# Four-pass graph network, 8-head pass: ScalarE weighs eight of sixteen tiles, and tail and query products stand elsewhere in TensorE's order

## The chip, the cores and the metric

The kernel runs on one core of a Trainium2 chip. The metric is the device time in microseconds of one execution, as a median of runs. Engines are named as in the profile: PE is TensorE (PEld its weight loads), DVE is VectorE, ACT is ScalarE, POOL is GpSimd, SP is SyncE.

## What is computed

Four graph layers in a row over 6250 nodes with 256 features and 106250 edges, sorted by destination. Each is followed by a residual sum and a layer norm. The second layer, which the change touches, is an 8-head attention over the edges (`q`, `k`, `v` are projections of the node features, `c` the destination and `r` the source of an edge):

```python
qe, ke, ve = q[:, c, :], k[:, r, :], v[:, r, :]
sim = jnp.einsum('hed,hed->eh', qe, ke) * scale
m = jax.ops.segment_max(sim, c, num_segments=bs)
p = jnp.exp(sim - m[c])
s = jax.ops.segment_sum(p, c, num_segments=bs)
attn = p / s[c]
out_e = attn.T[..., None] * ve
agg = jax.ops.segment_sum(out_e, c, num_segments=bs)
```

## The kernel before

The edges lie in 880 tiles of 128, each tile with destinations in one block of 128 nodes. Five passes (`L` = 0 to 4) go over the tiles; pass 1 is the 8-head pass. It takes the tiles in 55 batches of 16. The loop body of every engine is written out for two batches, and each body does two things: the scores of batch b ("scores"), and the weighted sums of batch c = b - 1 ("sums"). Each engine runs its instructions in the order of its body; semaphores tie the engines together. There is no planner.

What a batch needs, engine by engine:

- GpSimd gathers key and value rows (`kv_t`, 512 numbers) by edge source into `ring`, 16 tiles to a set, two sets; four tiles at a time, once TensorE has summed the four tiles that lay there.
- SyncE loads mask rows (`mk`, `srow`), the destinations as a row (`relx`), and query rows of the destination block, 128 x 256 bf16 (64 KB) a tile, into eight buffers `qw`. Tiles 8 to 11 of a batch are asked for when query products 0 to 3 of the batch are done, tiles 12 to 15 when products 4 to 7 are.
- TensorE spreads queries over edges: `dest_rows(b, par, r)` makes query products for four tiles (4r to 4r + 3), three matmuls a tile (lines 1042 to 1044; the third reads `qw`). It also makes the window sums: one matmul a tile with the one-hot destinations `ohc` (line 977), out of `add_tiles`, into one of three PSUM banks. Sum k waits for the add of tile k - 3, and at each fourth tile for the one-hots (`oc`) and the weighed values (`wv` from VectorE, `wa` from ScalarE).
- VectorE multiplies queries and keys of four tiles (line 1500), reduces to dot products (line 1491), then, after all four, runs a running maximum forward (`fw`, line 1526) and backward (`mx`, line 1532) along the edges of each tile, links tiles by rows on one partition (lines 1542 to 1569), and forms maxima and differences (1574 to 1591). In between it adds each window sum to the accumulator (line 1436), corrects the first window of a batch (1671, 1672), and weighs values with the exponentials: `weigh_four(g)` (line 1651) for tiles 4g to 4g + 3, g = 0, 1 and 2.
- ScalarE makes the one-hots of the sums, `hot_four(c, g)`, four tiles at a time (lines 766 and 769), weighs the values of tiles 12 to 15, 8 heads each, in 32 small activations (line 794), and takes the exponentials (812 to 820). Line 820, which makes `corr`, is the last step of a batch there; VectorE's `begin_sums` waits for it.

TensorE's small steps between the sums are `turn_scores` (1075), `rows_of` (heads, line 1086, and tails, 1087 and 1088, all gated by `ch1`, the backward scan), `cols_of` (1094, 1095, gated by `rows_before`), and `turn_back` (1100, 1101, gated by the exponentials). Its order in a body is: query products r = 2; sums 0 to 3; query products r = 3; sums 4 to 7; sum 8; turned scores; sum 9; heads and tails; sums 10, 11; query products r = 0 of the next batch; sums 12, 13; columns; sums 14, 15; query products r = 1 of the next batch; turn back.

## Time and profile before

| | us |
|---|---|
| median of 3 runs (6994.69 to 6996.19) | 6995.06 |
| the profiled execution | 6978.94 |
| its span, first to last instruction | 6977.1 |
| busy: PE / DVE / ACT / POOL | 4606.5 / 4396.6 / 2546.8 / 4515.6 |
| mean granted TensorE clock | 0.771 |

The 8-head pass lies between about 1480 and 3025 us of the span. A timeline lists instructions in order of time, like ones merged (x4 is four of them); in brackets stands how long the engine was idle before it and what released it. fp32 matmuls appear as two entries each. The granted clock is a share of 2.4 GHz.

### The profile page before, as it was taken

To read this page: it belongs to the slowest core of one execution; us is meant where nothing else is said; L and a number is where in the kernel's file an instruction comes from. 1 tells how busy PE (TensorE), PEld (TensorE's weight loads), DVE (VectorE), ACT (ScalarE), POOL (GpSimd) and SP (SyncE) were. 2 spreads that over 40 slices of the span, in tenths; PEclk is the share of its full clock that TensorE was granted. 3 is DMA by queue.
4 is the path that set the end of the run, shared out by engine and by line. 5 is a ranking of instruction groups with operands and counts; after the bars stand their busy time and mean duration, and the time that the engine had idled before them with its cause. 6 is when DMAs were issued, how large, how long until landed. Compare 5 with 4: busy or idle time off the path is not lost.

```text
span 6977.1 us, 103168 instructions
## 1 busy us (share of the span) xinstructions
PE 4606.5 (66%) x17172; PEld 3026.2 (43%) x17173; DVE 4396.6 (63%) x11645; ACT 2546.8 (37%) x6805; POOL 4515.6 (65%) x4928
## 2 busy tenths in 40 slices
PE   3555555877777777784777777566776735555556
PEld 2444444544444444463444444444444423343333
DVE  5555554558888888874666666655565564444546
ACT  0000000545555655654555555554554540000004
POOL 5777776036666666617777775377777747777770
PEclk8777777988888878896777777777777767777776
DMA  3333335257777777745444444344444543333333
GB/s 86 105 105 105 105 104 102 90 189 221 222 219 222 219 222 223 214 123 149 137 131 132 132 131 92 99 133 135 131 131 136 119 137 105 105 105 105 105 103 89
DMA packets 499186, 962.75 MB, mean 138 GB/s; under 512 B 105403, under 2 KB 296510, under 8 KB 491616
## 3 DMA queue, kind: packets, MB, share of 16 engines
q0 software_dynamic: 240064, 696.46, 36.9%
q1 hardware_dynamic: 258749, 262.93, 11.6%
q14 instruction: 335, 2.74, 0.1%
q8 instruction: 38, 0.62, 0.0%
HBM read 895.74 MB, written 64.63 MB: 138 GB/s over the span
## 4 chain that ended last, share of the span: by engine, by line
PE 36%; POOL 20%; issue 18%; DVE 15%; DVEq 4%; DMA 4%; ACT 3%; ACTq 1%; POOLq 0%; SPq 0%
PE bank L977 21%; POOL ring L707 19%; DVE acc L1439 4%; PE bank L1027 3%; DMA ring<-g_t,stage 2%; PE bank L1221 2%; DVE ring L1651 2%; DVE acc L1436 2%; PE bank L1174 1%; DVE aux L1500 1%; PE bank L1042 1%; DVE ohc L1445 1%; PE bank L1043 1%; PE bank L1044 1%; PE bank L1200 1%
## 5 line engine op out<-in xcount | busy, mean ns | idle before, releaser
L977 PE MATMUL bank<-ring,ohc 128*128 128x256 f32 (+3 forms) x8800 | 3212.4, 517 | 1550.7 <-DMA ring<-xs_t,stage 432.4
L977 PEld LDWEIGHTS bank<-ring,ohc 128*128 128x128 f32 x8800 | 2063.5, 252 | 2500.1 <-issue 1066.7
L1439 DVE TENSOR_TENSOR acc<-acc,bank 128x256 f32 (+2 forms) x3520 | 1485.2, 422 | 1498.3 <-PE bank L977 1368.0
L707 POOL DMA_INDIRECT ring<-g_t,stage x1760 | 1715.7, 975 | 521.7 <-issue 466.2
L707 POOL DMA_INDIRECT ring<-kv_t,stage x880 | 918.2, 1043 | 555.3 <-PE bank L977 325.8
L707 POOL DMA_INDIRECT ring<-in_x,stage x880 | 835.2, 949 | 263.8 <-issue 256.7
L707 POOL DMA_INDIRECT ring<-xs_t,stage x880 | 834.1, 948 | 260.9 <-issue 258.3
L840 ACT ACTIVATE aux<-bank 128x512 f32<-128x512 f32 (+1 forms) x26 | 14.9, 572 | 2225.5 <-PE bank L1163 2225.5
L766 ACT ACTIVATE ohc<-iota,rel_c 128x128 f32<-128x128 f32 x1760 | 557.2, 388 | 67.7 <-PE bank L977 66.6
L812 ACT ACTIVATE cl<-cl 128x1 f32<-128x1 f32 (+3 forms) x111 | 22.5, 203 | 1502.6 <-DVE mx L1644 909.7
L1436 DVE SCALAR_TENSOR_TENSOR acc<-acc,aux,bank 128x264 f32 x880 | 422.9, 481 | 119.9 <-PE bank L977 106.8
L1651 DVE TENSOR_TENSOR ring<-ring 128x1024 f32<-128x1024 f32 (+1 forms) x495 | 487.4, 985 | 14.1 <-issue 5.7
L794 ACT ACTIVATE ring<-ring 128x32 f32<-128x32 f32 x1760 | 378.1, 306 | 0.0
L1445 DVE TENSOR_SCALAR ohc<-iota,rel_c,relx 128x128 f32<-128x128 f32 x883 | 321.0, 364 | 88.3 <-issue 88.3
L827 ACT ACTIVATE ring<-ring 128x256 f32<-128x256 f32 x880 | 353.9, 493 | 2.2
L1448 DVE TENSOR_SCALAR ohc<-iota,rel_c 128x128 f32<-128x128 f32 x883 | 273.9, 310 | 99.4 <-issue 99.4
L769 ACT ACTIVATE ohc<-ohc,onesm 128x512 f32<-128x512 f32 x440 | 317.6, 722 | 32.3
L1042 PE MATMUL bank<-acc,oht 128*128 x880 | 268.2, 305 | 38.7 <-DMA aux<-q_t 30.0
L1500 DVE TENSOR_TENSOR aux<-bank,ring 128x1024 f32<-128x1024 f32 x220 | 267.9, 1218 | 11.6 <-PE bank L1044 10.0
L1491 DVE TENSOR_REDUCE sc<-aux 128x32 f32<-128x1024 f32 x220 | 267.3, 1215 | 2.0
L1043 PE MATMUL bank<-acc,oht 128*128 x880 | 266.7, 303 | 0.0
L1044 PE MATMUL bank<-aux,oht 128*128 128x256 bf16 x880 | 261.0, 297 | 0.0
(299 smaller groups left out, 4954.1 us busy)
## 6 DMA issues: line engine op xcount, KB each, us to landing
aux<-relb_t SPq DMA_DIRECT2D x56, 1024.0 KB
aux<-q_t SPq DMA_DIRECT2D x880, 64.0 KB
relx<-relb_t SPq DMA_DIRECT2D x55, 512.0 KB
ring<-g_t,stage POOLq DMA_INDIRECT x1760, 2.8
x<-ring SPq DMA_DIRECT2D x21, 896.0 KB, 4.2
ring<-x SPq DMA_DIRECT2D x21, 896.0 KB, 9.5
mk<-mk SPq DMA_DIRECT2D x445, 32.1 KB
ring<-in_x,stage POOLq DMA_INDIRECT x880, 2.8
```

What stands on the lines that cost most here:

```text
L707: g_.indirect_dma_start(out=rings[L][:, slot, 0:W], out_offset=None, in_=table[L][:, :], in_offset=bass.IndirectOffsetOnAxis(ap=stage[:, s ...
L766: act.activation(ohc[:, at_k + j, :], iota[:, :], ACT.Abs, scale=-1.0, bias=rel_c[:, ds(c * G + 4 * g + j, 1)])
L794: ins = act.activation(part, part, ACT.Copy, scale=rg[:, cset * G + k, po_ + h:po_ + h + 1])
L827: ins = act.activation(row, row, ACT.Copy, scale=rg[:, rset * G + k, 256:257])
L977: return mm(agp[k % AB][:, 0:width], ohc[:, hot, :], rg[:, slot, vo:vo + width], start=True, stop=True)
L1042: mm(to, hot, accb[:, ds(at_ + 2 * AW, D)], start=True, stop=False)
L1043: mm(to, hot, accb[:, ds(at_ + (2 * AW + D), D)], start=False, stop=False)
L1436: v.scalar_tensor_tensor(win, win, same[:, ds(b * G + k, 1)], agp[k % AGP[L]][:, 0:width], ALU.mult, ALU.add).then_inc(p["added"], 1)
L1439: tt(win, win, agp[k % AGP[L]][:, 0:width], ALU.add).then_inc(p["added"], 1)
L1445: ins = v.tensor_scalar(ohc[:, k % 8, :], iota[:, :], rel, ew_c[:, ds(b * G + k, 1)], ALU.is_equal, ALU.mult)
L1500: tt(prod, qe4[r % 2].rearrange("p (t w) -> p t w", t=4), rg[:, rset * G + 4 * r:rset * G + 4 * r + 4, 0:256], ALU.mult).then_inc(p["prod" ...
L1651: return tt(vv, vv, wv, ALU.mult)
```

## The change

In pass 1 alone:

- ScalarE weighs tiles 8 to 15 (64 activations, two increments of `wa`) where it weighed 12 to 15; VectorE's `weigh_four(2)` goes, and it adds tiles 1 and 2 in a row.
- ScalarE makes the one-hots of groups 0 to 2 of a batch one body earlier, behind the weighings and ahead of the exponentials; group 3 stays in the body of its sums, now at the head of it.
- TensorE makes the tails first, from the forward scan's last column and gated by it (`tails_of`), and the heads behind them, gated as before (`heads_of`).
- The next batch's query products r = 0 move from between sums 11 and 12 to behind sum 15; those of r = 1 move behind `turn_back`.
- The counts that passes 2 and 3 wait for (`weighed`) follow.

```diff
 def weighed(L):
-    return (0, 0, 3 * NB, 3 * NB + TS[2] // 4)[L]
+    return (0, 0, 2 * NB, 2 * NB + TS[2] // 4)[L]
...
-                        for g in range(min(hots, 3)):
-                            hot_four(c, g)
                         if L == 1 and sums:
-                            for k in range(12, 16):
+                            hot_four(c, 3)
+                        if L == 2:
+                            for g in range(min(hots, 3)):
+                                hot_four(c, g)
+                        if L == 1 and sums:
+                            for k in range(8, 16):
                                 for h in range(H):
                                     part = rg[:, cset * G + k, 256 + 32 * h:288 + 32 * h]
                                     ins = act.activation(part, part, ACT.Copy, scale=rg[:, cset * G + k, po_ + h:po_ + h + 1])
-                            ins.then_inc(p["wa"], 1)
-                        for g in range(3, min(hots, 4)):
-                            hot_four(c, g)
+                                if k % 4 == 3:
+                                    ins.then_inc(p["wa"], 1)
+                        if L == 1 and scores:
+                            for g in range(3):
+                                hot_four(b, g)
...
-                                if L == 1 and k < 12:
-                                    pe.wait_ge(p["wv"], b * 3 + (k // 4 + 1))
-                                if L == 1 and k == 12:
-                                    pe.wait_ge(p["wa"], b + 1)
+                                if L == 1 and k < 8:
+                                    pe.wait_ge(p["wv"], b * 2 + (k // 4 + 1))
+                                if L == 1 and k >= 8:
+                                    pe.wait_ge(p["wa"], b * 2 + (k // 4 - 1))
...
+                        def tails_of():
+
+                            gate(pe, p["fwd"], b + 1)
+                            mm(m1[0:1, tail:tail + HW], fw[0:R, 127:128], sel[0:R, 0:HW], start=True, stop=False)
+                            mm(m1[0:1, tail:tail + HW], ones[0:1, 0:1], fprow[0:1, fp_at, 0:HW], start=False, stop=True)
+
+                        def heads_of():
+
+                            gate(pe, p["ch1"], b + 1)
+                            mm(m1[0:1, head:head + R], mx[0:R, 0:1], ident[0:R, 0:R], start=True, stop=True)\
+                                .then_inc(p["row"], 1)
...
                             sums_of(9, 10)
                             if scores:
-                                rows_of()
-                            sums_of(10, 12)
-                            if feed:
-                                dest_rows(nb, npar, 0)
-                            sums_of(12, 14)
+                                tails_of()
+                                heads_of()
+                            sums_of(10, 14)
                             if scores:
                                 cols_of()
                             sums_of(14, 16)
                             if feed:
+                                dest_rows(nb, npar, 0)
+                            if scores:
+                                turn_back()
+                            if feed:
                                 dest_rows(nb, npar, 1)
-                            if scores:
-                                turn_back()
...
                             add(0, 1)
                             dots(1)
-                            add(1, 2)
-                            weigh_four(2)
-                            add(2, 3)
+                            add(1, 3)
                             pair(2)
```

## Rows read from the trace of the kernel before

**Rows 1.** Timeline of ScalarE over one cycle: start, length, line, operation.

```profile
2512.51 0.35 ACT L820 ACTIVATE corr<-bank,first_in 128x8 f32<-128x8 f32 x1
...
2518.73 6.87 ACT L794 ACTIVATE ring<-ring 128x32 f32<-128x32 f32 x32
2525.51 1.26 ACT L766 ACTIVATE ohc<-iota,rel_c 128x128 f32<-128x128 f32 x4
...
2527.57 0.28 ACT L809 ACTIVATE first_in<-oht,onesm 128x1 f32<-128x1 bf16 x1
...
2539.84 0.35 ACT L820 ACTIVATE corr<-bank,first_in 128x8 f32<-128x8 f32 x1
```

**Rows 2.** Busy time by stage: PE, PEld, DVE, ACT, POOL, granted clock, DMA share.

```profile
2520.00:2524.00 4.00, 1.90 (x7) 0.65 (x5) 4.00 (x7) 4.00 (x20) 3.34 (x3) 0.95 0.55 147
...
2529.00:2534.00 5.00, 5.00 (x20) 2.92 (x18) 3.39 (x11) 0.00 (x0) 2.58 (x3) 0.52 0.81 252
```

**Rows 3.** Waits, 1600 to 2900 us: total, times, longest.

```profile
DVE acc L1436 <- PE bank L977: 86.7, 48, 1.8
DVE rows L1542 <- PE bank L1088: 39.7, 48, 0.8
...
ACT cl L812 <- DVE mx L1591: 501.9, 48, 10.5
```

**Rows 4.** Timeline of VectorE in the same cycle.

```profile
2510.97 1.22 DVE L1500 TENSOR_TENSOR aux<-bank,ring 128x1024 f32<-128x1024 f32 x1
...
2519.39 1.22 DVE L1651 TENSOR_TENSOR ring<-ring 128x1024 f32<-128x1024 f32 x1
2520.52 0.48 DVE L1436 SCALAR_TENSOR_TENSOR acc<-acc,aux,bank 128x264 f32 x1
...
2537.97 0.28 DVE L1591 TENSOR_TENSOR mx<-bank,mx 128x128 f32<-128x128 f32 x1
2538.17 1.21 DVE L1500 TENSOR_TENSOR aux<-bank,ring 128x1024 f32<-128x1024 f32 x1
```

**Rows 5.** Timeline of TensorE, from the heads to the next batch's query products.

```profile
2528.67 0.58 PE L1086 MATMUL bank<-ident,mx 128*1 128x128 f32 x2 [0.25 <-DVE mx L1532]
...
2530.18 2.13 PE L977 MATMUL bank<-ring,ohc 128*128 128x264 f32 x4
2532.10 0.42 PE L1042 MATMUL bank<-acc,oht 128*128 x1
...
2535.23 0.38 PE L1094 MATMUL bank<-ones,rows 1*128 1x1 f32 x2
...
2536.76 0.27 PE L1042 MATMUL bank<-acc,oht 128*128 x1
...
2537.96 0.27 PE L1044 MATMUL bank<-aux,oht 128*128 128x256 bf16 x1
```

**Rows 6.** Requests for query rows (SPq), and the first product reading them.

```profile
1505.47 4.64 SPq L552 DMA_DIRECT2D aux<-q_t  x8
...
1511.05 0.39 PE L1042 MATMUL bank<-acc,oht 128*128 x1 [3.88 <-DMA aux<-q_t]
...
1525.03 5.54 SPq L552 DMA_DIRECT2D aux<-q_t  x8
...
1529.74 0.39 PE L1042 MATMUL bank<-acc,oht 128*128 x1 [0.89 <-DMA aux<-q_t]
...
2507.31 5.75 SPq L552 DMA_DIRECT2D aux<-q_t  x8
...
2512.64 0.10 PEld L1042 LDWEIGHTS bank<-acc,oht 128*128 128x128 bf16 x1 [0.44 <-issue]
```

**Rows 7.** One batch near the pass's end: line 820 twice, and the stage.

```profile
2949.42 0.35 ACT L820 ACTIVATE corr<-bank,first_in 128x8 f32<-128x8 f32 x1
...
2974.78 0.35 ACT L820 ACTIVATE corr<-bank,first_in 128x8 f32<-128x8 f32 x1
...
2949.00:2975.00 26.00, 18.15 (x97) 12.05 (x96) 24.30 (x44) 16.22 (x61) 16.58 (x17) 0.93 0.97 191
```

More of the change, by code:

```diff
@@ L794, in chain @@
                                     ins = act.activation(part, part, ACT.Copy, scale=rg[:, cset * G + k, po_ + h:po_ + h + 1])
-                            ins.then_inc(p["wa"], 1)
-                        for g in range(3, min(hots, 4)):
-                            hot_four(c, g)
+                                if k % 4 == 3:
[3 more added lines that the diff above has]
+                                hot_four(b, g)
+                        if L == 2:
+                            for g in range(3, min(hots, 4)):
+                                hot_four(c, g)
                         if feed and L > 1:
                             hot_turned(b + 1, (o + 1) % 2)
-                        for g in range(4, hots):
+                        for g in range(4, hots if L == 2 else 0):
                             hot_four(c, g)
@@ L1126, in batch @@
                             if feed:
-                                dest_rows(nb, npar, 1)
+                                dest_rows(nb, npar, 0)
                             if scores:
                                 turn_back()
+                            if feed:
+                                dest_rows(nb, npar, 1)
                         else:
```

## The prediction, made before the change was run

> **What bounds the kernel now.** The change touches only the 8-head pass (55 batches of 16 tiles, 54 steps from one to the next), so I first looked at how regular that pass is. ScalarE's last step of a batch (line 820) starts at 2512.51 and again at 2539.84: a cycle of 27.33 us [rows 1]. All of the 54 intervals but a few at either end are 27.3 us, so one cycle stands for the pass: a microsecond per cycle is 54 us, or 0.8% of the time.
>
> The stages of the cycle come next [rows 2]. While VectorE alternates key products, dot products and window adds it is busy for 4.00 of 4.00 us and TensorE for only 1.90; then the granted clock falls from 0.95 to 0.52 (about the lower of its two levels, 1.2 of 2.4 GHz) and stays there through heads and tails and sums 10 and 11. There TensorE is busy for 5.00 of 5 us and VectorE for 3.39: it waits. The waits say for what [rows 3]: 86.7 us in 48 batches (1.81 each) for a window sum, 39.7 (0.83 each) for the tail product. ScalarE waits 501.9 us (10.5 each) for VectorE's last difference, so it has room. The cycle is thus VectorE's order of work, plus two waits for a TensorE at its lower clock.
>
> **The change, part by part.** I set P = 2510.97, where VectorE starts a batch's first key product [rows 4], and give times behind P.
>
> 1. *VectorE no longer weighs tiles 8 to 11.* The step at 2519.39 goes and the add at 2520.52 moves up [rows 4]: 1.13 us, on the path, since VectorE has no idle time there [rows 2].
>
> 2. *ScalarE weighs tiles 8 to 15.* 32 weighings run from 2518.73 to 2525.51, 6.78 us; 64 are 13.56. A set of four one-hots and the short step behind it take 2527.57 - 2525.51 = 2.06 [rows 1], the set alone at most 2.0. The new order behind a cycle's line 820 is one set, 64 weighings, three sets and two short steps: 13.56 + 8.0 + 0.4 = 22.0 us. Now it works 6.8 less up to the same point, and then waits 10.5 [rows 3]. From VectorE's difference (ends 2538.25) to the end of line 820 (2540.19) are 1.94 [rows 1, 4], so ScalarE alone would carry a cycle of 23.9. The wait that the change adds is TensorE's, at tiles 8 and 12, with all later products of TensorE behind it. Tiles 8 to 11 are weighed at P + 1.9 + 2.0 + 6.78 = P + 10.7, tiles 12 to 15 at P + 17.5. Sum 8, the turned scores and sum 9 stand ahead of the heads (2528.67 now), some 3 us of work at the low clock, so sum 8 starts at about 2525.7 now and at P + 13.6 then; sum 12 not before sum 11's end, 2532.10 [rows 5], P + 19.7 with what is saved ahead of it. Both are covered, by 3 and 2 us. The one-hots for the next batch wait for sums 3, 7 and 11, all past by then. Cost: nothing. Were the cover gone, each microsecond late would be one on the cycle.
>
> The Trainium skill, page "ScalarE: Activation LUTs", section "Rules for kernel authors", budgets about 0.3 us for each activation and 0.83 ns per element; by that 64 weighings are some 21 us, ScalarE would carry the cycle at 31 and the change would lose 200 us. The trace has 32 in 6.78 us, 0.212 each, in every cycle, so I give it no chance.
>
> 3. *Tails before heads.* TensorE makes the tail row when the forward scan is done and fills the gap in front of the heads: it idled 0.25 us before 2528.67 [rows 5]. Gain 0.25 at the lower clock; at the full clock up to the whole 0.83 of the wait.
>
> 4. *Query products of the next batch, four tiles, move from in front of sum 12 to behind sum 15.* Sums 10 and 11 take 0.96 each at the low clock (2530.18 to 2532.10). The columns' products now start at 2535.23; with only sums 12 and 13 ahead of them they start at 2532.10 + 1.92 = 2534.02: 1.21 earlier, and VectorE's chain up to the last difference (2.4 us further on) with them. In exchange the next batch's first key product needs what was moved. Behind that start come the columns and sums 14 and 15 (2535.23 to 2536.76, 1.53) and the four query tiles (2536.76 to the end of the twelfth product, 2537.96 + 0.27: 1.47) [rows 5]: ready at 2537.0 on the old scale, where VectorE would be ready at 2538.17 - 1.21 = 2536.96. Cost 0.25 with the semaphores. That is at the full clock; if the clock is still low there, the same products take twice as long, some 2.2 more (two sums 1.0, twelve products 1.2).
>
> So far: 27.33 - 1.13 - 0.25 - 1.21 + 0.25 = 24.99.
>
> 5. *What hangs on the move.* SyncE loads the query rows of tiles 8 to 11 as soon as these query products are done with the buffers. Now it asks at 2507.31 and TensorE needs them at 2512.64, 5.33 later, without a wait. After the change the request goes out at about P + 0.1, and TensorE is through with turning back and the other four query tiles at about P + 2.9. How long do these rows (64 KB for a tile) take? Where TensorE did wait, it started 1511.05 - 1505.47 = 5.58 and 1529.74 - 1525.03 = 4.71 behind the first request [rows 6]. I take 5.2, nearer the steady 5.33 that sufficed: TensorE idles 2.3 us, its products for tiles 8 to 11 end at P + 6.7, and sums 0 to 2, queued behind them, start there. The first window add could start at P + 6.5 (nothing ahead of it is saved); sum 0 is read at about P + 7.4. Cost 0.9 at the full clock. At the lower clock these twelve take twice as long, 1.2 us more, and the cost is 2.1. The rows of tiles 12 to 15 and the mask rows queued behind on SyncE start some 3 us later than now, and are used 5 and 10 us later: nothing.
>
> The sum: 24.99 + 0.9 = 25.9 us per cycle.
>
> 6. *The clock* is the term that I can't read off. At the full clock there is one witness: the batch from 2949.42 to 2974.78, with granted clock 0.93 over it, took 25.36 us [rows 7], although its query rows came late. Less the 1.13, that is 24.2; with the late rows' remaining 0.1, 24.3. The change makes the stretch of thin TensorE work shorter (one VectorE step fewer in it, and late query products pushed towards it), which speaks for a clock that falls less often; and it opens a new gap of 2.3 us, which speaks against. I keep "low around heads and sums 10 to 13, full again for what is moved", which is nearest to what the stages show today [rows 2]: 25.9.
>
> **The sum.** 54 x (27.33 - 25.9) = 77 us. The profiled execution took 6978.94 us (span 6977.1), 16 below the median of the runs, 6995.06. Taken off the profiled time it gives 6902, off the median 6918; I predict the median.
>
> **The rivals.**
> - *The clock stays up.* 24.3 a cycle, 54 x 3.0 = 163 saved: 6832. For it: that one batch [rows 7]. Against: its work was spread by late loads in a way no other batch shows. Chance 0.12.
> - *Query rows come in time.* If they land within 2.7 us of the request, step 5 costs nothing: 24.99, 54 x 2.3 = 126 saved: 6869. Both waits [rows 6] speak against it. Chance 0.08. The Trainium skill, page "DMA: Bandwidth & Descriptors", section "Anatomy of one DMA — SWDGE (gpsimd) path", fits a transfer at about 2.0 us plus its bytes over 436 GB/s (for GpSimd's path; SyncE's starts a little sooner): an estimate of 2.2 us for 64 KB, which would be this rival; the trace's 4.7 to 5.6, beside a stream of gathers, disagrees.
> - *The saving is eaten, no change.* The new gap lowers the clock once more, before the query products of tiles 8 to 11: 24.99 + 2.1 = 27.1, and with a few tenths for ScalarE or late rows 27.3: 6995. Chance 0.14.
> - *Slower.* One mechanism: TensorE's clock is low both behind the new gap and through sums 14, 15 and the moved query products, since each stretch of full work is now followed by a wait. Cost 2.1 and half of 2.2 (some batches): 24.99 + 3.2 = 28.2, so 54 x 0.87 = 47 us more: 7042. It decides from 27.33 - 24.99 = 2.3 us of such cost on. For it: TensorE at 1.90 of 4 us was enough to lose the clock [rows 2]. Against: behind the columns TensorE has 2.3 to 4.5 us of work without a gap, as it has today before the clock is back. Chance 0.18.
> - *ScalarE becomes the bound.* It sets a floor of 23.9 and would only cap the first rival; it has no chance of its own.
>
> **How the numbers follow.** My forecast (25 to 27 a cycle, 6870 to 6978) has 0.48. Faster by over 0.2% (14 us, about what a measurement can tell from no change) is 0.48 + 0.12 + 0.08 = 0.68; within it 0.14; slower 0.18. For eight times in ten the range reaches to 24.5 a cycle below (leaving out half of the first rival) and to 27.6 above (leaving out most of the slower one): 6842 to 7010.
>
> **What would show it.** In the profile after: VectorE without a weighing between the adds of tiles 1 and 2 (step 1); ScalarE's wait for the last difference down from 10.5 to some 3 us, and no wait of TensorE for ScalarE's weighings (step 2); the waits for the tail product and the window sum gone or small, replaced by one for the columns (steps 3, 4); a new wait of TensorE for query rows of about 2.3 us, and VectorE waiting for sum 0 (step 5); the granted clock near 0.5 once in a cycle, around the heads, and nearly 1 elsewhere (step 6). The prediction is wrong if the cycle is over 27 us, which would be the clock, or if TensorE waits for ScalarE.

## The result and the profile after

The changed kernel takes 7005.09 us (median of 20 runs, 6993.93 to 7013.63), the kernel before 6992.59 beside it. The ratio is 1.0017, 95% interval 1.001 to 1.0024: slower by 0.17%, clear of noise but less than the 0.2% that the prediction called no change. Forecast was 6918. That 7005 still lies in the range of 6842 to 7010 is due to its ends, which were stretched for the rivals; the forecast missed by 87 us. The profiled run took 7001.0 us, its span is 6999.2.

The length of the 8-head pass did not move. From its first query product to its last are 1488.2 us before (1502.5 to 2990.7) and 1489.5 after (1506.3 to 2995.8), and the mean distance of one batch's turned scores to the next's is 27.34 us in both (median 27.41 before, 27.12 after). So VectorE dropped a weighing per batch and the batch stayed as long on average.

Over 1600 to 2900 us the two traces read as follows (busy time of PE, PEld, DVE, ACT, POOL, then granted clock, DMA share, GB/s). Before:

```profile
1600.00:2900.00 1300.00, 1000.23 (x4485) 612.73 (x4485) 1129.37 (x2049) 752.37 (x2792) 819.23 (x810) 0.81 0.74 221
```

After:

```profile
1600.00:2900.00 1300.00, 1037.58 (x4506) 651.46 (x4504) 1094.32 (x2010) 1084.87 (x4340) 771.06 (x813) 0.78 0.74 222
```

VectorE has 35 us less work, TensorE 37 us more busy time for the same work, at a lower clock. The waits of the same stretch in the kernel after (total, times, longest), against [rows 3]:

```profile
PE bank L1050 <- DMA aux<-q_t: 130.8, 84, 3.7
...
DVE acc L1456 <- PE bank L985: 65.6, 107, 2.1
DVE mx L1594 <- PE bank L1115: 41.5, 48, 1.1
DVE aux L1520 <- PE bank L1052: 31.4, 24, 1.5
DVE rows L1562 <- PE bank L1100: 25.8, 45, 0.7
...
ACT cl L820 <- DVE mx L1611: 127.3, 48, 3.3
```

VectorE's waits for the window sum and for heads and tails shrank (86.7 to 65.6, 39.7 to 25.8), but two stand beside them that were 12.2 us and nothing before: for the columns (L1115) and for the moved query products (L1052). TensorE waits 130.8 us for query rows, 2.7 for each of 48 batches. ScalarE's wait for the last difference fell from 501.9 to 127.3 us (10.5 to 2.7 a batch). TensorE is never listed as waiting for ScalarE's weighings.

One batch on TensorE, from the late query rows to the next batch's query products (start, length, line, operation, idle time before it). L985 are window sums, L1094, L1095 the tails, L1100 the heads, L1114, L1115 the columns, L1120, L1121 turn back:

```profile
2537.71 0.28 PE L1050 MATMUL bank<-acc,oht 128*128 x1 [1.68 <-DMA aux<-q_t]
...
2547.81 1.25 PE L985 MATMUL bank<-ring,ohc 128*128 128x264 f32 x2 [0.82 <-DVE acc L1456]
...
2550.51 0.61 PE L1094 MATMUL bank<-sel_b,fw 128*1 128x136 f32 x2
2551.05 0.61 PE L1095 MATMUL bank<-fprow,ones 1*1 1x136 f32 x2
2551.59 0.59 PE L1100 MATMUL bank<-ident,mx 128*1 128x128 f32 x2
2552.11 3.89 PE L985 MATMUL bank<-ring,ohc 128*128 128x264 f32 x8
2555.93 0.58 PE L1114 MATMUL bank<-ones,rows 1*128 1x1 f32 x2
2556.38 0.56 PE L1115 MATMUL bank<-ones,rows 1*128 1x1 f32 x2
2556.86 2.13 PE L985 MATMUL bank<-ring,ohc 128*128 128x264 f32 x4
2558.79 0.42 PE L1050 MATMUL bank<-acc,oht 128*128 x1
...
2561.20 0.27 PE L1120 MATMUL bank<-ident,fw 128*128 128x128 f32 x1
```

And the same time in stages, with the granted clock (third from the end):

```profile
2544.00:2547.00 3.00, 1.43 (x4) 0.60 (x4) 3.00 (x5) 3.00 (x15) 2.39 (x3) 1.00 0.71 194
2548.00:2551.00 3.00, 3.00 (x7) 1.08 (x7) 2.70 (x6) 3.00 (x15) 2.39 (x3) 0.50 0.95 310
2551.00:2554.00 3.00, 3.00 (x9) 1.68 (x9) 2.48 (x7) 2.85 (x9) 1.32 (x2) 0.50 0.87 272
2554.00:2557.00 3.00, 3.00 (x10) 2.07 (x8) 1.66 (x8) 2.80 (x8) 1.71 (x2) 0.50 0.78 247
2557.00:2560.00 3.00, 3.00 (x10) 2.10 (x11) 2.32 (x7) 0.01 (x1) 2.14 (x3) 0.50 0.68 186
2562.00:2564.00 2.00, 0.92 (x9) 0.58 (x6) 1.97 (x3) 1.93 (x6) 1.39 (x3) 1.00 0.87 221
```

Here is what failed. The clock falls where it fell before, in the stage in which VectorE bounds the work and TensorE has 1.43 us to do in 3. In this batch it does not come back with the sums behind the heads: it is 0.50 through heads, columns, sums 14, 15 and the moved query products (12 us, though TensorE is busy all the time). In the kernel before it was back when the columns started at 2535.23, two of them in 0.38 us and two query products 0.27 long [rows 5]; here they take 0.58 and 0.42.

But not every batch of the changed kernel is like this one. The batch just before it, with the longer wait for query rows, its sums 0 to 3, then sums 10 to 13 and the columns:

```profile
2511.58 0.28 PE L1050 MATMUL bank<-acc,oht 128*128 x1 [3.17 <-DMA aux<-q_t]
...
2513.32 3.68 PE L985 MATMUL bank<-ring,ohc 128*128 128x264 f32 x8
...
2526.36 3.89 PE L985 MATMUL bank<-ring,ohc 128*128 128x264 f32 x8
2530.18 0.42 PE L1114 MATMUL bank<-ones,rows 1*128 1x1 f32 x2
```

```profile
2513.30:2516.60 3.30, 3.30 (x10) 2.54 (x9) 2.02 (x4) 3.30 (x17) 0.00 (x0) 0.50 0.36 86
2530.40:2533.00 2.60, 2.60 (x20) 2.20 (x20) 2.02 (x7) 0.58 (x3) 1.93 (x2) 1.00 0.77 222
```

Here the clock dips behind the new wait (0.50 over sums 0 to 3, which take 3.68 us; in the batch of 2537.71 the same four take 2.15), and around the heads it is low for a shorter time, so that it is full for sums 14, 15 and the moved products. The two kinds alternate. Between 1600 and 2900 us the changed kernel's clock has 24 long low stretches (some 14 us, as in the first listing) and 20 short ones around the heads (some 7 us), each with one of some 3 us ahead of it; together it is low for 556 us, in the kernel before for 481, in 47 stretches of some 10 us each.

I read it so that each kind brings on the other. Where the moved products are late, turning back is ready right behind them, TensorE is through with its next query products 1.3 us behind the request for rows (2507.07 to 2508.40) and waits 3.17 us; where they are in time, it waits for turning back first, is through 2.6 us behind the request (2533.45 to 2536.03) and waits 1.68. That this wait decides on the clock around the heads is not shown. So the mean of 27.34 stands for no single batch; from one first key product to the next it is about 26.5 and 28.1 in turn.

VectorE in the batch of the first listing, behind its long low stretch:

```profile
2555.39 0.49 DVE L1456 SCALAR_TENSOR_TENSOR acc<-acc,aux,bank 128x264 f32 x1
2556.97 0.36 DVE L1594 SCALAR_TENSOR_TENSOR mx<-mk,bank,mx 128x128 f32<-128x128 f32 x1 [1.10 <-PE bank L1115]
...
2559.67 0.28 DVE L1611 TENSOR_TENSOR mx<-bank,mx 128x128 f32<-128x128 f32 x1
...
2561.40 1.22 DVE L1520 TENSOR_TENSOR aux<-bank,ring 128x1024 f32<-128x1024 f32 x1 [1.44 <-PE bank L1052]
```

From the columns to VectorE's last difference are now 3.74 us (2555.93 to 2559.67), before 2.74 (2535.23 to 2537.97 [rows 4, 5]): 1.0 lost in such a batch, 0.55 on average over 48 (3.28 for 2.73). And the next key product waits 1.44 us for the moved query products, in 24 of 48 batches, 0.65 each on average.

### The profile page after: what moved, and what is told of

Read it like the earlier page. It is cut to its first block, busy times and chain, and to the rows that moved or that the text cites. A ratio compares the mean times of both kernels' runs of the same rounds, so it can differ in the third digit from the quotient of the medians.

```text
span 6999.2 us, 104928 instructions
## 1 busy us (share of the span) xinstructions
PE 4624.8 (66%) x17172; PEld 3060.0 (44%) x17173; DVE 4346.6 (62%) x11590; ACT 2923.0 (42%) x8565; POOL 4472.8 (64%) x4928
## 4 chain that ended last, share of the span: by engine, by line
PE 37%; POOL 20%; issue 17%; DVE 12%; DMA 6%; DVEq 4%; ACT 2%; SPq 1%; POOLq 0%; ACTq 0%
PE bank L985 23%; POOL ring L707 19%; DVE acc L1459 4%; DMA aux<-q_t 3%; PE bank L1035 3%; DMA ring<-g_t,stage 2%; PE bank L1241 2%; DVE ohc L1465 1%; PE bank L1194 1%; PE bank L1050 1%; PE bank L1051 1%; DVE acc L1456 1%; PE bank L1052 1%; DVE ring L1671 1%; SPq L552 1%
## 5 line engine op out<-in xcount | busy, mean ns | idle before, releaser
L985 PE MATMUL bank<-ring,ohc 128*128 128x256 f32 (+3 forms) x8800 | 3241.4, 525 | 1408.5 <-DMA ring<-xs_t,stage 413.0
L985 PEld LDWEIGHTS bank<-ring,ohc 128*128 128x128 f32 x8800 | 2125.7, 258 | 2334.9 <-issue 983.3
L707 POOL DMA_INDIRECT ring<-g_t,stage x1760 | 1734.1, 985 | 521.7 <-issue 471.5
L707 POOL DMA_INDIRECT ring<-kv_t,stage x880 | 863.1, 981 | 609.2 <-PE bank L985 364.6
L797 ACT ACTIVATE ring<-ring 128x32 f32<-128x32 f32 x3520 | 751.0, 306 | 0.0
L1671 DVE TENSOR_TENSOR ring<-ring 128x1024 f32<-128x1024 f32 (+1 forms) x440 | 420.1, 955 | 9.5
L1050 PE MATMUL bank<-acc,oht 128*128 x880 | 258.4, 294 | 174.9 <-DMA aux<-q_t 170.3
L1087 PE MATMUL bank<-ident,sc 128*128 128x128 f32 (+3 forms) x112 | 36.6, 427 | 345.9 <-DVE sc L1539 345.9
L1051 PE MATMUL bank<-acc,oht 128*128 x880 | 258.0, 293 | 0.0
```

The lines of the kernel that those rows point to most:

```text
L707: g_.indirect_dma_start(out=rings[L][:, slot, 0:W], out_offset=None, in_=table[L][:, :], in_offset=bass.IndirectOffsetOnAxis(ap=stage[:, s ...
L797: ins = act.activation(part, part, ACT.Copy, scale=rg[:, cset * G + k, po_ + h:po_ + h + 1])
L985: return mm(agp[k % AB][:, 0:width], ohc[:, hot, :], rg[:, slot, vo:vo + width], start=True, stop=True)
L1050: mm(to, hot, accb[:, ds(at_ + 2 * AW, D)], start=True, stop=False)
L1051: mm(to, hot, accb[:, ds(at_ + (2 * AW + D), D)], start=False, stop=False)
L1671: return tt(vv, vv, wv, ALU.mult)
```

## The experiments

Two points on how to read them. First, the chips were in different condition. For one group of them (and for the result above) the kernel before takes 6992 us, for the four other groups 8381 to 8512 us, with waits of TensorE that the trace can attribute to nothing ("issue": 56.7 us in 63 waits over 1000 us of the changed kernel). A ratio is always against the kernel before on the same chip, and I call the first chip undisturbed and the others stalling. Second, 0.1% is 7 to 8 us, or 0.14 us per batch.

### Which part of the change costs what

Weighing alone (the changed kernel with TensorE's order of before):

```
-                            sums_of(10, 14)
+                            sums_of(10, 12)
+                            if feed:
+                                dest_rows(nb, npar, 0)
+                            sums_of(12, 14)
```

(and heads, tails, turn back and the query products r=1 at their old places).

> The changed kernel with TensorE's order of before (heads and tails together, query products r = 0 ahead of sum 12, r = 1 ahead of turning back); only the weighing of tiles 8 to 11 and the one-hots are moved. CLOCK theory (the lower TensorE clock ends only when bf16 query products run, and the changed order brings them 5 us of sums later): the clock is low for about 10 us a cycle as before, the cycle falls by the 1.13 us of the weighing to about 26.2 us, time about 6935. LATE ROWS theory (the new wait of 2.7 us for query rows ate the gain): the same, since the wait is gone here. HELD theory (a shorter VectorE order gives nothing, the cycle is held by something else): 27.3, time within 10 us of before.

Measured: 8296.41 us against 8385.33, ratio 0.9899, interval 0.988 to 0.9917.

The new order alone (the kernel before with only TensorE's new order):

> The kernel before with only TensorE's new order (tails before heads, query products r = 0 behind sum 15, r = 1 behind turning back); VectorE still weighs tiles 8 to 11. CLOCK and LATE ROWS: slower than before by some 1 us a cycle, 28.2, about 7045 (the changed kernel's cycle of 27.1 plus 1.13). CLOCK: low clock for 13 us a cycle. If the order is neutral: 27.3, within 10 us of before.

Measured: 8405.32, ratio 1.0034, 1.0019 to 1.0048. That is slower, but by less than half of what both theories had (7045, ratio 1.0075). TensorE waits there 133.9 us for query rows in 49 waits between 1900 and 2900 us.

The weighing part was measured three more times, each time on a stalling chip again, so its gain on an undisturbed chip is not shown:

> ScalarE's and VectorE's part of the change alone, TensorE in the order of the kernel before (query products r=0 ahead of sum 12), the same kernel as weigh-only, now on a chip where the kernel before takes 6992 us. CLOCK: the query products bring the clock back ahead of sums 12 to 15 and VectorE's order is 1.1 us shorter: faster than before by 0.4 to 1.0% (6922 to 6965 us). Rival WEIGH (the shorter VectorE order gives nothing here, the gain of 1% belonged to the other chip): 6985 to 7000 us.

> ScalarE's and VectorE's part of the change alone, TensorE in the order of the kernel before, once more. On the chips where the kernel before takes 8385 and 8502 us it measured 0.990. If this chip is one where the kernel before takes 6992 us: NARROW (the query products lie between heads and columns as before and bring the clock back; VectorE's order is 1.1 us shorter, part of it lost to other waits) 0.992 to 0.997; rival WEIGH (a shorter VectorE order gives nothing on an undisturbed chip) 0.999 to 1.001.

Measured: 8410.22 against 8501.77, ratio 0.9897 (0.9874 to 0.992), and 8439.52 against 8512.2, 0.9914 (0.9895 to 0.9934). The last time it ran beside the changed kernel itself:

> The changed kernel itself, unaltered, on the same chip as the run of its weighing part alone, so that what the new TensorE order costs can be read as the difference of two ratios. NARROW: the new order takes back all that the weighing gains, 1.000 to 1.006 times the kernel before, 0.7 to 1.4% above the weighing part alone, with the clock low for longer in each step. Rival (the parts add up as they measured alone, 0.990 and 1.003): 0.992 to 0.995.

> ScalarE's and VectorE's part of the change alone, TensorE in the order of the kernel before, beside the changed kernel on one chip. NARROW: 0.988 to 0.993 where the chip stalls as in the runs before (kernel before at 8385 to 8512 us), 0.992 to 0.997 where it takes 6992 us. Rival WEIGH (nothing on an undisturbed chip): 0.999 to 1.001 there.

Measured on one chip, kernel before at 8381.2 us: changed 8419.35, ratio 1.0035 (1.0019 to 1.0051); weighing alone 8294.85, 0.9884 (0.9867 to 0.9901). So VectorE's and ScalarE's part is a gain of 1.2%, 86 us or 1.6 per batch, and the new TensorE order takes back 1.5% (125 us, 2.3 per batch) when it is added to it, though it costs only 0.34% alone. The parts do not add up (0.992 would be the product). I read it so that the weighing's gain needs an order in which TensorE delivers. The 1.6 per batch is more than the 1.13 of VectorE's work that went; where the rest comes from on these chips is not shown.

On an undisturbed chip the changed kernel once more, and the kernel before against itself:

> The changed kernel, unaltered, beside the other kernels of this group on one chip. CLOCK and LATE ROWS theories: its ratio to before is that of the order alone (1.0034) times that of the weighing alone (0.990), 0.993 to 1.002; the first measurement gave 1.0017.

> The kernel before, unaltered: its profile on the chip of this group, to compare stages of the 8-head pass and of the unchanged passes. Ratio 1.000 to within 0.003.

Measured: 7008.27 against 6991.93, ratio 1.0023 (1.0013 to 1.0032); kernel before against itself 1.0001 (0.9991 to 1.0011). The profile of this second run shows the same alternation, with 24 long low stretches, 23 short ones around the heads and 24 of some 3 us.

### Late query rows

Sixteen buffers for query rows in place of eight, the order of the change kept:

```
-    qw = aux[:, 0:1024] ... k=8
+    qw = aux[:, 0:2048] ... k=16
...
-    sp.wait_ge(p["qe"], b * 4 + (k // 4 + 1))
+    wait(sp, p["qe"], b * 4 + (k // 4 - 1))
```

> The changed kernel with 16 query buffers instead of 8, so that all query rows of a batch are asked for a batch ahead and no query product waits for them. LATE ROWS: the wait of 2.7 us is gone and with it what ate the gain: cycle 25.5 to 26.2, time 6915 to 6950. CLOCK: the low stretch stays at about 13 us up to the query products behind sum 15, VectorE gets back only its wait of 0.6 us for sum 0; cycle 26.5 or more, time 6965 to 7000.

> The changed kernel with sixteen buffers for query rows in place of eight, so that the rows are there when the products want them; the order of the change is kept. LATE ROWS: the wait of 2.7 us a step for query rows was what ate the gain: 54 steps of up to 2.7 us, 6860 to 6900 us. CLOCK: the half clock of 13 us a step is still there and takes part of it back: 6940 to 6990 us, with the mean clock of the pass at or below that of the changed kernel (0.78).

Measured: 8279.61 against 8385.33, ratio 0.9874 (0.9856 to 0.9891); and 8414.71 against 8501.77, 0.99 (0.9877 to 0.9923). The first lies beyond what LATE ROWS gave (6915 to 6950, ratio 0.989 to 0.994), the second between the two theories. TensorE waits in the changed kernel (third run) for query rows, first line; with sixteen buffers there is no such line. The stages from 1900 to 2900 us of both (changed, then sixteen buffers):

```profile
PE bank L1050 <- DMA aux<-q_t: 107.1, 48, 7.0
...
1900.00:2900.00 1000.00, 751.46 (x3010) 462.51 (x3011) 730.66 (x1351) 732.35 (x2911) 507.21 (x545) 0.72 0.66 193
```

```profile
1900.00:2900.00 1000.00, 778.22 (x3191) 476.96 (x3191) 767.02 (x1424) 782.63 (x3080) 532.99 (x576) 0.74 0.69 205
```

With the rows there, 6% more products of TensorE (3191 for 3010) are done in the same 1000 us, and the new order is as good as the old one (0.9874 and 0.99 against 0.9899 and 0.9897 on the same two chips), although the mean clock is still 0.74 against 0.78 with the old order. So on stalling chips it is the late rows that eat the gain: 1.0035 to 0.9874 is 1.6%, 2.5 us per batch (two stalling chips, 8381 and 8385 us for the kernel before), although the clock is still low at the columns in 37 of 39 batches. Both runs fell on stalling chips, so neither this size nor that the rows alone suffice is shown for the undisturbed one.

The query products r=0 back in front of sum 12 and r=1 in front of turning back, tails still first:

> The changed kernel (tails first, weighing moved) with the query products r = 0 back ahead of sum 12 and r = 1 back ahead of turning back. CLOCK: low stretch about 10 us, cycle 26.2 less the 0.25 of the tails: 25.9 us, time about 6920, and sums 12 to 15 at the full clock. If tails first is worth nothing, the same as e1.

Measured: 8315.71, ratio 0.9921 (0.9902 to 0.994). Moving the query products back is enough: the loss is in step 4 of the prediction and what hangs on it. Tails before heads do not cause it, and gain nothing that can be told from noise (0.9899 without them). With sixteen buffers on top, on the undisturbed chip:

> e3 (weighing moved, tails first, query products r = 0 ahead of sum 12 and r = 1 ahead of turning back) with 16 query buffers. LATE ROWS theory: there is no wait for query rows in this order, so buffers give nothing, same as e3 (ratio 0.992 on the first chip). CLOCK theory: the best of all, with the clock back early, 0.985 to 0.992.

Measured: 6966.94, ratio 0.9965 (0.9952 to 0.9979). It beats both kernels, though by less than either theory had (0.992, and 0.985 to 0.992). Its pass takes 1461.7 us and the mean batch 26.79; the clock of the stretch is up at 0.83:

```profile
PE bank L985 <- DVE acc L1457: 132.8, 148, 1.1
PE bank L985 <- DVE ring L1672: 47.5, 37, 1.5
...
1900.00:2900.00 1000.00, 774.92 (x3520) 481.21 (x3520) 847.32 (x1574) 846.13 (x3390) 618.34 (x635) 0.83 0.75 226
```

Further forward, in front of sum 10, they do harm:

> The kernel with query products r=0 ahead of sum 12 and sixteen buffers (6967 us, 26.73 us a step), with these products moved on to stand ahead of sum 10. CLOCK: the bf16 products bring the clock back about two sums earlier, so sums 10 and 11 or 12 and 13 run in 1.06 us for two in place of 2.13 us: 0.5 to 1.2 us a step less, 6900 to 6940 us. Rival ORDER (the place of the products within the sums is indifferent so long as they come before the columns, or they only hold the sums up): 6960 to 6985 us.

Measured: 8597.52 against 8501.77, ratio 1.0113 (1.0089 to 1.0136). Both theories missed it. TensorE now waits for VectorE's weighing step ahead of the sums, 190.5 us in 27 waits against 18 to 48 us in the runs above that weigh on ScalarE and have these products elsewhere:

```profile
PE bank L985 <- DVE ring L1671: 190.5, 27, 8.1
```

and VectorE for its part waits 167.8 us, in 27 waits, for ScalarE's last step (line 828). Why ScalarE ends later there I did not settle.

### The clock

After the first traces I held that only the bf16 query products bring the clock back, since it rose 1.4 to 2.3 us behind their start in the batches that I had read. The other kind of batch in the changed kernel speaks against it already: there it rose by 2530.40, with heads and window sums ahead and the query products still to come. The test is to put spare products between sums 11 and 12 of the changed kernel:

```
+    gate(pe, p["seen"], b + 1)
+    for k in range(12):
+        mm(m1[:, 128:384], oht[:, par, 128 * k:128 * k + 128], oht[:, par, 0:256], ...)
```

> The changed kernel with twelve spare bf16 matmuls of 256 columns, as large as the moved query products, put between sums 11 and 12 (behind the rows' forward step; their result is read by nobody). CLOCK theory: bf16 products in the low stretch bring the clock back some 5 us earlier, so sums 12 to 15 and the query products run at the full clock; the 2.5 us of added work are repaid, cycle 27.1 to 27.6, time within 25 us of the changed kernel. If the kind of the products does not matter: the clock comes back no earlier, and 2.5 us of TensorE work lie on the path to the columns' product, cycle 29, time 100 us above the changed kernel.

Measured on the undisturbed chip: 7024.04, ratio 1.0044 (1.003 to 1.0058), 0.2% above the changed kernel beside it. The spare work is 2.14 us per batch up to the next sum, and the batch grew by 0.35 (27.40 to 27.75): most of it is repaid, since sums and columns behind it are at the full clock, two sums in 1.06 us instead of 2.13, the columns so in all of the 47 batches read:

```profile
2514.59 2.13 PE L985 MATMUL bank<-ring,ohc 128*128 128x264 f32 x4
2516.51 2.30 PE L1107 MATMUL bank<-oht 128*128 128x256 bf16 x12
2518.65 1.06 PE L985 MATMUL bank<-ring,ohc 128*128 128x264 f32 x4
2519.63 0.38 PE L1120 MATMUL bank<-ones,rows 1*128 1x1 f32 x2
```

That fits my reading, but it does not test the number type. The control has six fp32 products, 128*128 by 128 columns, of the same TensorE time:

```
-    for k in range(12):
-        mm(m1[:, 128:384], oht[:, par, 128 * k:128 * k + 128], oht[:, par, 0:256], ...)
+    for k in range(6):
+        mm(m1[:, 128:256], ident[:, :], iota[:, :], ...)
```

> The changed kernel with six spare fp32 products of 128 columns between window sums 11 and 12 of each step of the 8-head pass; their result goes nowhere. It is the control of the run with twelve spare bf16 products in the same place (7024 us, 27.57 us a step, the clock full again behind them). Six fp32 products of 128 columns are 1.28 us of TensorE at the full clock and 2.56 us at half, the bf16 ones were 1.28 and 2.56 too. Theory CLOCK (fp32 work does not bring the clock back, bf16 work does): the clock stays at half through the spare products and sums 12 to 15, nothing is repaid, the step is longer than that of the changed kernel (27.14 us) by 2.0 to 2.6 us, time 7110 to 7145 us. Rival FILL (any TensorE work in that place brings it back, or the place was a pause in disguise): like the bf16 ones, 7015 to 7035 us, sums 12 to 15 at 1.06 us for two.

Measured: 8540.91 against 8501.77, ratio 1.0044 (1.0026 to 1.0062), where my theory wanted 1.017 to 1.022. In the trace the clock is back behind the fp32 products too, at the columns in 25 of 36 batches, where the changed kernel on a stalling chip has it back in 5 of 36:

```profile
2518.52 2.13 PE L985 MATMUL bank<-ring,ohc 128*128 128x264 f32 x4
2522.04 2.90 PE L1107 MATMUL bank<-iota,ident 128*128 128x128 f32 x12 [1.39 <-DVE rows L1573]
2524.73 1.14 PE L985 MATMUL bank<-ring,ohc 128*128 128x264 f32 x4
```

The theory of the bf16 products fell. Read again, all traces have something else in common: wherever the clock stayed low although TensorE was busy, products of one row or onto one row (tails, heads, columns) lay among the sums. They lie there in the batches in which it came back too, so this can be a part of the cause at most. The next control keeps the six products, their 128 columns, their place and their type, and makes them 1*1:

```
-        mm(m1[:, 128:256], ident[:, :], iota[:, :], ...)
+        mm(m1[0:1, 128:256], ident[0:1, 0:1], iota[0:1, :], ...)
```

> The changed kernel with six spare fp32 products between window sums 11 and 12 of each step, 128 columns each as in the run with spare fp32 products, but of a single row onto a single row (1*1) in place of 128*128; their result goes nowhere. With 128*128 fp32 products in this place the clock was back in the step that was read behind them (2524.73, two sums in 1.14 us), so that it is not the number type that decides. Theory NARROW: products of one row or onto one row (tails, heads, columns) do not help to bring the clock back although TensorE is busy with them, and the changed order lays them so that less work of full width stands between them. Then the clock stays at 1.2 GHz through these spare products and, in most steps, through sums 12 and 13 (2.13 us for the two), the mean clock of the pass is at or below that of the changed kernel (0.78) and the step is 1.8 to 2.6 us longer than its own: 1.014 to 1.022 times the kernel before. Rival FILL (any product in that place does it): the clock is back at sum 12 as with the twelve bf16 products, mean clock 0.80 to 0.83, 1.002 to 1.007 times the kernel before. Neither number depends on the chip; where the chip stalls, the clock at sums 12 and 13 decides.

Measured: 8652.16 against 8512.2, ratio 1.0166 (1.0143 to 1.0189), in the range that NARROW had given:

```profile
2512.79 2.13 PE L985 MATMUL bank<-ring,ohc 128*128 128x264 f32 x4
2515.89 2.71 PE L1107 MATMUL bank<-iota,ident 1*1 1x128 f32 x12 [0.96 <-DVE rows L1573]
2518.53 2.13 PE L985 MATMUL bank<-ring,ohc 128*128 128x264 f32 x4
2520.59 0.58 PE L1120 MATMUL bank<-ones,rows 1*128 1x1 f32 x2
2521.03 0.56 PE L1121 MATMUL bank<-ones,rows 1*128 1x1 f32 x2
2521.53 2.13 PE L985 MATMUL bank<-ring,ohc 128*128 128x264 f32 x4
```

The spare products take as long as before (2.71 for 2.90), the sums and columns behind them are all at half speed, the columns so in all of the 34 batches read. The stages from 1900 to 2900 us, spare fp32 first, one-row second:

```profile
1900.00:2900.00 1000.00, 745.49 (x3298) 486.01 (x3297) 715.07 (x1313) 720.53 (x2855) 507.36 (x532) 0.77 0.64 188
```

```profile
1900.00:2900.00 1000.00, 785.12 (x3149) 478.27 (x3148) 682.53 (x1251) 672.50 (x2686) 484.73 (x508) 0.70 0.61 179
```

The two kernels differ in nothing but the rows of these products, and by 1.2% (on two stalling chips, 8502 and 8512 us for the kernel before): about 103 us, 1.9 per batch. On stalling chips, that is the price of the clock staying low behind sum 11, measured by itself. The full-width ones cost 0.1% over the changed kernel (1.0044 against 1.0035, on different chips), the thin ones 1.3%.

Does making one thin product of the kernel full-width help? All 128 columns of the scanned rows as weights of the heads product:

```
-    mm(m1[0:1, head:head + R], mx[0:R, 0:1], ident[0:R, 0:R], ...)
+    mm(m1[:, head:head + R], mx[0:R, 0:128], ident[0:R, 0:R], ...)
```

> The changed kernel with the heads product made of full width: all 128 columns of the scanned rows stand as weights in place of the first alone, so that row 0 of the result is the same as before and rows 1 to 127 go nowhere; the number of streamed columns and the waits are unchanged. NARROW: the work of full width between the tails and the columns grows by 0.6 us (heads and sums 10 to 13, 4.1 us at 1.2 GHz in place of 3.5), so the clock comes back ahead of the columns in part of the steps: mean clock of the pass up by 0.01 to 0.04, step 0.3 to 1.0 us shorter, ratio 0.994 to 0.999. Rival (the width of a product is nothing to the clock): the same as the changed kernel within 0.1%, ratio 1.001 to 1.003 where the chip is undisturbed.

> The fastest version so far (ScalarE and VectorE as changed, query products r=0 ahead of sum 12, sixteen buffers for query rows; ratio 0.9965) with the heads product of full width too. NARROW: the clock comes back with heads, sums 10, 11 and the query products, some steps one stretch earlier: ratio 0.990 to 0.996. Rival (width is nothing to the clock): 0.995 to 0.998.

Measured: 8553.73 against 8512.2, ratio 1.004 (1.0024 to 1.0057), beside 1.0035 for the changed kernel, and a clock of 0.72 from 1900 to 2900 us in both; and 8429.98 against 8512.2, 0.9903 (0.9882 to 0.9924), in the range of 0.990 to 0.996 but on a stalling chip, where no kernel differs from it by the heads alone (query products ahead of sum 12 with eight buffers stand at 0.9921, sixteen buffers with the new order at 0.9874 and 0.99), so it says nothing for it. In the first the rival held: 0.6 us more of full width, with the tails still in front and the columns behind, move nothing. So what is shown is that with 2.3 to 2.9 us of full-width work more between sums 11 and 12 the clock was back at the columns (always with bf16, in 25 of 36 batches with fp32), and with 2.7 us of one-row work in none of 34; how much more of full width the changed order would need, I have not measured.

## Why the prediction was wrong, step by step

The sizes below are means over the 48 batches between 1600 and 2900 us, after against before, read at VectorE's steps.

1. *VectorE drops a weighing, -1.13.* Right in kind, smaller in size: the two adds stood 1.53 us apart (2518.99 and 2520.52) and now stand 0.66 apart, since the second waits a little for the first; from the first window add to the forward scan VectorE takes 9.05 in place of 9.92: -0.87. In whole runs, this part alone gives 0.9884 to 0.9914 in four runs, all on stalling chips.
2. *ScalarE's weighings are covered.* Right: 64 of them take 13.65 us (forecast 13.56), its wait is down to 2.7 a batch, 3.3 at most (forecast "some 3"), TensorE never waits for them. The prediction had sums 3, 7 and 11 past when the next one-hots want them; sum 11 is not in about half of the batches (ScalarE waits 37.7 us in 25 waits), but this lies within ScalarE's spare time. The row of the Trainium skill that the prediction named, page "ScalarE: Activation LUTs", section "Rules for kernel authors", gives an estimate of 21 us for 64 activations; in the trace one lasts 0.306 us, but they start 0.213 apart.
3. *Tails before heads, -0.25.* Right in size: from the forward scan to the first step on the rows it is 2.78 in place of 3.05, -0.27.
4. *Query products behind sum 15, -1.21 and +0.25.* The columns start 3.82 us behind sum 10 (2552.11 to 2555.93) in place of 5.05 (2530.18 to 2535.23 [rows 5]): 1.23 earlier, as forecast, in both kinds of batch. But the columns, the differences behind them and the moved products were priced at the full clock, and in about half of the batches they run at 0.50. From the first step on the rows to the last difference the gain is then 0.74 on average and not 1.21, and the key product comes 0.95 behind the last difference in place of 0.26: 0.69 for the forecast 0.25. The prediction named 2.2 "if the clock is still low there" and then did not take it.
5. *Late query rows, +0.9.* The mechanism is there, and TensorE idles 2.7 us for them (forecast 2.3). The first window add starts 7.61 behind the batch's first key product, before 6.50 (2517.47 and 2510.97): 1.1 on the undisturbed chip. On stalling chips it was mis-sized: 2.5 per batch by the runs with sixteen buffers.
6. *"Low around heads and sums 10 to 13, full again for what is moved."* This is the step that failed. The prediction has the clock fall once in a cycle and be back for the moved products. In 24 of 48 batches it stays low for some 14 us, up to the end of the moved products or nearly so, and in most others it falls twice, behind the new gap and around the heads: low for 11.8 us a batch in place of 10.2. The belief was read off a kernel in which these very products stood between sums 11 and 12, and the change took them away from there. The witness for a clock that stays up [rows 7] was weak as well: its batch of 25.36 us is followed by one of 30.74 (line 820 again at 3005.52).

Summed: -0.87 - 0.27 - 0.74 + 0.69 + 1.11 = -0.08 per batch, where the prediction had -1.13 - 0.25 - 1.21 + 0.25 + 0.9 = -1.44. Of the missing 1.36, 0.91 is the clock (step 4 by way of step 6), 0.26 the weighing and 0.21 the late rows, less 0.02 that the tails gave more. This sum of intervals must close; what it shows is where the time went, not what each cause would give back by itself. The rival "the saving is eaten, no change" (27.3, 6995, chance 0.14) came true in its number and in half of its mechanism: its dip behind the new gap is there in about half of the batches, and in the other half stands the clock that stays low through columns, sums and moved products, which the prediction had kept for the slower rival.

The remaining 10 to 15 us are not in the 8-head pass. From the first to the last turned scores of the following pass, whose order the change doesn't touch, are 1146.1 and 1150.6 us in two profiles of the kernel before, and 1157.7, 1160.7, 1160.2 and 1162.1 in those of the changed kernel (twice), spare products and the sixteen-buffer version. All four have the new weighing, but profiled runs scatter (that of the sixteen-buffer version is 11 us above its median, and its median gain of 25 us is just the 26 us by which its 8-head pass is shorter), so this may be a small effect or chance. It was not tested and stays open.

Open as well: how the loss divides between rows and clock on the undisturbed chip. There the two were only undone together (0.9965); the division above is read from waits and starts, not from a run. Since the length of the wait for rows and the kind of the low stretch go together batch by batch, the two may not be separable there. Not shown either is why the clock comes back before the columns in one batch and not in the next.

## What to carry to other kernels

Before moving work out of a stretch, ask what it does there for others: with the query products between heads and columns TensorE's clock was back at the columns in all of 48 batches, without them in 17 of 48, and their place also set when eight buffers came free. Cost the moved work, and everything between its old place and its new one, at the lower clock too, and give the buffers a turn of their own before changing the order. Read two batches in a row, and the count of low stretches over the pass, before taking one for all: here the kinds alternated. Parts of a change that gain alone (0.988) and lose little alone (1.003) can lose together (1.0035), so each part is worth a run.

## What the runs showed of the hardware

- Six fp32 products of 128 rows and six of one row, in the same place and of nearly the same length, did not stand alike with the clock: behind the first (2.90 us) it was back at the columns in 25 of 36 batches, behind the second (2.71 us) in none of 34. TensorE "busy" for 3.00 of 3 us was thus no sign that the clock would rise. The Trainium skill, page "TensorE: Matmul & The Clock Gate", section "What's actually happening", has it that the chip sets the clock by how busy the engine has been; the busy time in these profiles does not tell the two kernels apart.
- A clock pattern can span two batches: in the changed kernel one long low stretch (some 14 us) alternates with two short ones (some 3 and 7 us), in a loop whose work is the same each time.
- Query rows (64 KB a tile) were read 4.3 us behind the first request, on the undisturbed chip, as soon as they had landed (requested at 2533.45, first product at 2537.71), below the 4.7 to 5.6 of [rows 6]:

```profile
2533.45 4.74 SPq L552 DMA_DIRECT2D aux<-q_t  x8
```

- The same kernel took 6992 us on one chip and 8381 to 8512 us on others, with the common instructions as long as on the other (984 against 987 ns for a gather's issue on GpSimd, 422 ns for VectorE's window add in both, each in the later passes), but with waits that nothing in the trace explains. Ratios differed too: on the stalling chips the changed kernel stood at 1.0035, on the undisturbed one at 1.0017 and 1.0023.
